# Expert stage of a GNN and routed-FFN kernel: TensorE transposes six of the eight payload pieces, VectorE the other two in squares of 32 lanes, ScalarE copies all six

## The reference

```python
def _L0_ffn_ref(x, W1, b1, Wg, bg, Wd, bd):      # C = 256, HID = 1024, 8 experts
    H = jax.nn.gelu(xf @ W1 + b1, approximate=False)
    probs = jax.nn.softmax((H @ Wg + bg) / TEMP, axis=-1)
    assign = jnp.argmax(probs, axis=-1)
    for e in range(Wd.shape[0]):
        y = H @ Wd[e] + bd[e]
        sel = (assign == e)[:, None]
        out = out + jnp.where(sel, probs[:, e:e + 1] * y, 0.0)
...
x = x + _L0_gnn_ref(_layernorm(x, axis=-1), ...)
x = x + _L0_ffn_ref(_layernorm(x, axis=-1)[None], ...)[0]
```

## Time and profile before

| what | value |
|---|---|
| median of three runs | 4533.39 us |
| profiled execution, its own time | 4543.27 us |
| its span | 4541.5 us |
| TensorE busy (matmuls) | 3492.5 us, 77% of the span |
| VectorE busy | 2074.2 us, 46% |
| ScalarE busy | 1219.3 us, 27% |
| GpSimd busy | 3294.1 us, 73% |
| expert stage, from the first payload gather to the end | from 4062.7 us on |

### The profile page before, as it was taken

How to read it: one execution, slowest core, us unless ns; L and a number is a source line. 1 busy time by engine, 2 the same in 40 slices (tenths; PEclk the granted TensorE clock), 3 DMA queues, 4 the chain that set the end, 5 groups by cost and what they waited for, 6 DMA issues and landing times.

```text
span 4541.5 us, 84544 instructions
## 1 busy us (share of the span) xinstructions
PE 3492.5 (77%) x21407; PEld 3281.8 (72%) x21408; DVE 2074.2 (46%) x7215; ACT 1219.3 (27%) x2041; POOL 3294.1 (73%) x3464
## 2 busy tenths in 40 slices
PE   4666777677677676668888878888887888779998
PEld 4565666666666666668878778778787887768887
DVE  8874343333333333335554544444554445463333
ACT  6652110000000000004333333333333333251111
POOL 6777777777777777767777777777777777716665
PEclk7667775666666666659888888898888888889999
DMA  5654443333333333334444444444444444445554
GB/s 183 195 187 116 118 118 114 112 113 111 113 113 111 112 113 111 113 95 133 146 146 144 142 147 145 142 145 146 144 144 142 148 145 142 138 151 180 180 179 145
DMA packets 248032, 626.83 MB, mean 138 GB/s; under 512 B 66279, under 2 KB 113014, under 8 KB 247358
## 3 DMA queue, kind: packets, MB, share of 16 engines
q0 software_dynamic: 173664, 491.88, 37.8%
q1 hardware_dynamic: 69646, 103.75, 6.4%
q10 hardware_dynamic: 4176, 26.61, 1.6%
HBM read 519.22 MB, written 103.73 MB: 137 GB/s over the span
## 4 chain that ended last, share of the span: by engine, by line
POOL 28%; PE 14%; issue 11%; DMA 2%; DVE 1%; ACT 1%; POOLq 0%; DVEq 0%; ACTq 0%; SPq 0%
POOL rows L550 28%; PE pA L1535 7%; PE pA L1382 2%; PE pB L1423 1%; DMA rows<-h_scratch,idx 1%; PE pC L1525 1%; PE pB L1525 1%; PE pC L1405 1%; ACT aggT L784 0%; DMA aggT<-pay_scratch,ids 0%; POOLq L365 0%; PE pZ L1392 0%; DVE S L928 0%; PE pT L1512 0%; POOLq L367 0%
## 5 line engine op out<-in xcount | busy, mean ns | idle before, releaser
L1382 PE MATMUL pA<-S,rows 128*128 128x96 f32 x12544 | 2084.0, 339 | 968.6 <-DMA rows<-xn_scratch,idx 398.4
L1382 PEld LDWEIGHTS pA<-S,rows 128*128 128x128 f32 x12544 | 1977.8, 250 | 1082.8 <-issue 409.7
L550 POOL DMA_INDIRECT rows<-h_scratch,idx x1564 | 1493.5, 955 | 493.2 <-issue 469.3
L550 POOL DMA_INDIRECT rows<-xn_scratch,idx x1296 | 1231.1, 950 | 395.1 <-issue 388.7
L928 DVE TENSOR_SCALAR S<-iota_p,tdst,twgt 128x96 f32<-128x96 f32 x3168 | 810.1, 351 | 11.8 <-issue 11.7
L979 DVE TENSOR_TENSOR aggT<-aggT,pA 128x192 f32 x784 | 278.3, 355 | 1034.8 <-PE pA L1382 774.4
L1031 DVE TENSOR_TENSOR zb<-pZ,brow 128x256 f32<-128x256 f32 x198 | 84.1, 425 | 852.3 <-issue 581.5
L1423 PE MATMUL pB<-work,w 128*128 128x128 f32 x3232 | 387.7, 278 | 0.0
L1535 PE MATMUL pA<-aggT,work 128*128 x1680 | 382.1, 381 | 0.0
L1423 PEld LDWEIGHTS pB<-work,w 128*128 128x128 f32 x3232 | 371.3, 193 | 0.0
L643 ACT ACTIVATE stage<-aggT 128x256 f32 x196 | 81.7, 417 | 1076.5 <-PE pZ L1392 644.6
(11 more groups left out here) (200 smaller groups left out, 2611.9 us busy)
## 6 DMA issues: line engine op xcount, KB each, us to landing
pay_scratch<-work SPq DMA_DIRECT2D x98, 512.0 KB
rows<-h_scratch,idx POOLq DMA_INDIRECT x1564
rows<-xn_scratch,idx POOLq DMA_INDIRECT x1296, 2.8
work<-in_x_dram ACTq DMA_DIRECT2D x15, 896.0 KB, 5.5
xn_scratch<-work ACTq DMA_DIRECT2D x14, 896.0 KB
h_scratch<-work SPq DMA_DIRECT2D x98, 128.0 KB
pay_scratch<-work SPq DMA_DIRECT2D x98, 128.0 KB
work<-in_x_dram SPq DMA_DIRECT2D x97, 128.0 KB
```

The lines of the kernel that those rows point to most:

```text
L550: pool.indirect_dma_start(rows[:, s, t, :], None, source, bass.IndirectOffsetOnAxis(at, 0))\
L1382: last = mm(to[:, k * W:(k + 1) * W], rows[:, slot, t, k * P:(k + 1) * P], Sx[:, t, :], start=(t == 0), stop=(t == T - 1))
```

## The change

TensorE transposes only the first ONPE = 6 pieces of a tile. ScalarE copies all six from PSUM. VectorE no longer copies from PSUM. Instead it takes the last two pieces straight from the gathered payload in SBUF and transposes them itself. Its transpose works on squares of 32 lanes by 32 columns, so that a 128 x 128 piece is 16 squares, each moved from one group of 32 lanes (i) to another (j). One instruction moves the square (i, j) of both pieces, 2 x 32 columns on 32 lanes, and so there are 16 instructions for one tile.

```diff
+    ONPE = 6
+    SQ = 32
...
             def copy_half(t, b2):
                 act.wait_ge(s_eT, t + 1)
                 act.wait_ge(s_y, t + 1)
-                act.activation(HTx[:, b2, 0:KH // 2, :],
-                               (pB, pC)[b2][:, 0:512].rearrange("p (k n) -> p k n", k=KH // 2),
+                act.activation(HTx[:, b2, 0:ONPE, :],
+                               (pB, pC)[b2][:, 0:ONPE * P].rearrange("p (k n) -> p k n", k=ONPE),
                                ACT.Copy).then_inc(s_eTa, 1)
...
-            def copy_half(t, b2):
-                dve.wait_ge(s_eT, t + 1)
-                v.tensor_copy(HTx[:, b2, KH // 2:KH, :],
-                              (pB, pC)[b2][:, 512:1024].rearrange("p (k n) -> p k n", k=KH // 2)).then_inc(s_eTd, 1)
+            def transpose_rest(t, q, nth, b2):
+                dve.wait_ge(s_pg[q], 16 * nth)
+                dve.wait_ge(s_y, t + 1)
+                rest = payx[:, q, ONPE * P:HID].rearrange("p (m h) -> p m h", m=KH - ONPE)
+                for i in range(P // SQ):
+                    for j in range(P // SQ):
+                        last = v.transpose(HTx[j * SQ:(j + 1) * SQ, b2, ONPE:KH, i * SQ:(i + 1) * SQ],
+                                           rest[i * SQ:(i + 1) * SQ, :, j * SQ:(j + 1) * SQ])
+                last.then_inc(s_eTd, 1)
...
-            copy_half(0, 0)
+            transpose_rest(0, 0, 1, 0)
...
-                    copy_half(t + 1, (r + 1) % 2)
+                    transpose_rest(t + 1, (q + 1) % QB, 2 * i + (r + 1) // QB + 1, (r + 1) % 2)
...
             def transpose_tile(i, q):
                 pe.wait_ge(s_pg[q], 16 * (i + 1))
-                for m in range(KH):
+                for m in range(ONPE):
```

## The result

The changed kernel took 4600.85 us in the median of four runs (4599.73 to 4604.22), the kernel before 4533.50 us (4531.38 to 4534.84). The ratio is 1.0152, with a 95% interval of 1.0141 to 1.0164: 67.35 us slower. The profiled execution took 4599.73 us, its span is 4598.0 us.

The account below looks back on a forecast made before the run. TensorE's work on each tile was taken as the bound, 4.35 us; serial squares would make VectorE the bound at 5.13 us. Over 103 tiles that adds 80.3 us to 4533.4, giving 4614 us, range 4506 to 4690.

Parts of the forecast that it names:

- TensorE's side: Two transposes less per tile save 0.217 us, 22.5 us over 104 tiles; a tile bound by TensorE would take 4.11 us.
- ScalarE's side: Its copy grows from 0.60 to 0.81 us a tile but is needed 3.5 us later, so it costs nothing.
- VectorE's cycle: VectorE's time per tile: 1.00 us of other work plus 16 squares, 5.13 us in sum, against 4.35 per tile before.
- S: Time from one VectorE square's start to the next, bounded between 0.13 and 0.30 us and taken as 0.258 us.
- the serial end: Each square starts only when the one in front has finished, 0.214 to 0.30 us apart; chance 0.68.
- rival 1: VectorE's squares overlap, 0.13 us apart, and TensorE stays the bound: 4511 us; chance 0.19.
- The table load: Load in front of VectorE's output, expected to run ahead behind the squares: 0, with 0.27 us a tile as the bound.
- Rival 4: The load in front of VectorE's output is exposed: +0.27 us a tile, +28 us, 4642 us; counted within the serial case's 0.68.
- TensorE's wait: TensorE needs 4.11 us a tile and so waits about 1.0 us a tile for VectorE before the product.
- The ends: Start and end of the expert stage: first squares over by 4076, first output waits until 4077.9 anyway; nothing added.
- Rival 2: Squares serial but at the low end of durations, 0.20 to 0.214 us apart: 4518 to 4541 us; chance 0.04.
- rival 3: Serial squares with a 4-byte transpose at half the stream rate, or a falling clock: +191 us, 4724 us; chance 0.09.

Follow-up runs that it names:

- e5: Changed kernel with VectorE only signalling, without a single square, so two of eight pieces keep old values: 4511.62 us against 4533.16 for the kernel before.
- e1b: Changed kernel with the square loops swapped, so each square reads from another lane group and every fourth writes to another: 4603.29 us, ratio 1.0159 to the kernel before.
- e2b: Changed kernel with all 16 squares reading and writing lanes 0 to 31, product input partly wrong: 4510.58 us, ratio 0.9952 to the kernel before.
- e3: Changed kernel with each square reading and writing the same lane group, the group changing after every four: 5651.03 us on a slower chip, ratio 1.0051.
- e4: Changed kernel with plain copies in place of the transposes, on the same lanes: 5619.09 us on a slower chip, ratio 0.9989 to the kernel before.
- e8: Changed kernel with VectorE transposing three pieces of odd tiles only, 96-column squares, six one tile early: 4519.15 us, ratio 0.9971 to the kernel before.
- e7: Changed kernel with VectorE transposing two pieces of odd tiles only, all 16 squares in the gap before their product: 4547.18 us, ratio 1.0034.
- e9: Changed kernel with VectorE transposing four pieces of odd tiles only, 128-column squares, six one tile early: 4524.59 us, ratio 0.9981 to the kernel before.

## Why the prediction was right

The forecast was 4614 us, within 4506 to 4690, and slower; it is 4600.85 us.

**What bounded the kernel before**, TensorE's work on a tile, holds. e5 takes two transposes away and the tile is 4.143 us; 4.11 had been forecast, and with the same 0.02 us of hiccups as in the 4.35 it is 4.13.

**TensorE's side**, 22.5 us, is 21.5 us (e5).

**ScalarE's side**, nothing: the copy takes 810 ns as forecast, and in e5, where VectorE is out of the way, no time is missing. What the waits put down to ScalarE is a matter of naming, as shown above.

**GpSimd's side**, nothing: the gather waits longer for its indices, 1.70 us in a tile for 0.78 before, and TensorE waits 0.4 us for a payload from 4080 us on.

**VectorE's cycle**, 1.00 + 16 S: output and indices take 0.93 to 1.00 us, and the sum holds within 0.05 us: 1.00 + 16 x 0.249 = 4.98, and 5.025 is measured, of which 0.02 are the waits once a round and 0.01 the step from the last square to the output (0.031 us in place of 0.014).

**S, the serial end.** The choice rested on the lane changes. e1b, e2b and e3 show this: without them it is 0.13 us and the time is that of rival 1 (4510.58 for 4511), with them on either side 0.249. The Trainium skill ("VectorE: DVE Perf Modes", "Two Vector instructions with no wait between them") has the instruction wait until all earlier ones have finished; the traces agree, with 0.249 us from start to start at a duration of 0.235. Its 311 ns in "The three transpose paths" gave an estimate of 0.244 us, and 0.249 was measured.

**The size of S** is the term that was off. Forecast was the middle of 0.214 to 0.30 us, 0.258, and it is 0.249. 16 x 0.009 x 103 = 15 us, against 13 us by which the forecast was too high. The middle included up to 0.04 us of passing on from one instruction to the next, read from a pair with a real wait between them; a square that is held behind another shows only 0.249 - 0.235 = 0.014 us. That the measured value lies so near the middle is in part luck: the rows bounded S to 0.09 us, which is 142 us over the stage, and the middle was a choice.

**The table load** was taken as 0, and no tile shows it: behind the 16 squares the output starts at once. Rival 4 has no share.

**TensorE's wait** was to be about 1.0 us a tile: 5.025 - 4.143 = 0.88.

**The ends.** From the first transposes to the first output it is 4053.95 to 4064.20, 10.25 us for 10.21 before; the squares of tiles 0 and 1 were over 2.20 us ahead of that output, about the 1.9 us that the forecast gave them. Nothing is added there, as forecast.

**Rivals 2 and 3.** Rival 2 needed a start before the reported end of the one in front and an S of at most 0.214 us. A square starts 0.014 us after that end, and S is 0.249. Its other condition, that reading a square first costs nothing, stays open: e4 has a transpose 0.050 us over a copy, without showing why. For rival 3, columns cost (0.249 - 0.215) / 32 = 1.06 ns each, the rate of the two-input instructions in the earlier trace rows, and the clock stayed at 1.00 with TensorE idle 13% of the stage.

What isn't settled: where the fixed 0.182 us of a held square lie within VectorE, for which these traces have only starts and durations; what a transpose does in the 0.050 us that it takes more than a copy; why two copies in each tile of e4 end together with GpSimd's DMA instructions; and why the squares start 0.23 us late once in a round, which costs 2.3 us and which no experiment touched.

## What to carry to other kernels

Before moving work to an idle engine, divide its idle time by the time from start to start of the new instructions in their real order, and look at which lanes each reads and writes: here 16 small instructions that change lanes took 4.0 us to save TensorE 0.217. When such instructions can't be avoided, make them few and wide, as in e8, where a column cost 1.05 ns and an instruction 0.182 us. Then check the chain as well as the sum, since an engine with enough idle time can still be late when its work stands behind something that itself waits (e7, e9).

## What the runs showed of the hardware

- A VectorE transpose of 64 columns started 0.249 us after the one in front when its input or its output began in another group of 32 lanes, and 0.13 us after it when both stayed; it makes no difference which of the two changed (e1b, e2b, e3). Copies are held as well, at 0.199 us. Two of 16 lasted until one of GpSimd's DMA instructions ended, about 0.3 us, and transposes did not (e4).
- Held transposes cost 0.215, 0.249, 0.282 and 0.316 us at 32, 64, 96 and 128 columns of 4 bytes: 0.182 us and 1.05 ns a column. The Trainium skill ("Vector Engine (DVE) Microarchitecture Reference", "The reshape front-end and per-opcode configuration") calls moves of 32 partitions to another group free, in a table of which groups an instruction may write. In time they are not: e2b against e1b shows that each such move in a row of them costs 0.12 us of overlap.
- The reported duration of one and the same instruction depends on what stands ahead: 235 ns where it was held and 193 where it wasn't. A sum of durations gave 16 x 0.193 = 3.1 us where the engine needed 2.1. Only the starts tell the throughput.
- With TensorE idle once in each 5 us, for 0.55 to 1.0 us by its rows, the granted clock was 1.00 in each 100 us from 4100 to 4500.
